# Last layer: two of eight channel blocks multiplied by the tokens' factors on POOL, six on VectorE

## The reference, cut to what matters

```python
def act_quant(x):
    scale = 127.0 / jnp.clip(jnp.max(jnp.abs(x), axis=-1, keepdims=True), 1e-05)
    return jnp.clip(jnp.round(x * scale), -128, 127) / scale
def bit_linear(x, w):
    ...
    return jnp.einsum('bsd,hd->bsh', xq, wq)
h = bit_linear(x, w1)
h = depthwise_conv1d(h.transpose(0, 2, 1), conv_w, conv_b)
h = h.transpose(0, 2, 1)
h = jax.nn.silu(h)
return bit_linear(h, w2)
```

## Time and profile before

| | us |
|---|---|
| median of 3 runs | 2888.92 |
| lowest, highest | 2888.0, 2890.59 |
| the profiled execution, device time | 2885.63 |
| its span in the trace | 2883.9 |
| DVE busy in the span | 1946.5 |
| PE busy | 2387.5 |
| POOL busy | 815.9 |

### The profile page before, as it was taken

The page is one execution under the profiler, slowest core; times in us unless marked ns, Lnnn a source line. Parts: engine busy times, 40 slices in busy tenths (PEclk is TensorE's granted clock), DMA queues, the critical chain, the costliest instruction groups (busy, mean ns, idle before and its releaser), DMA issues. The chain is left out here.

```text
span 2883.9 us, 43402 instructions
## 1 busy us (share of the span) xinstructions
PE 2387.5 (83%) x16438; PEld 1959.8 (68%) x16438; DVE 1946.5 (67%) x4381; ACT 1510.7 (52%) x2574; POOL 815.9 (28%) x712
## 2 busy tenths in 40 slices
PE   4778888876689999999868999999999367777665
PEld 2445555554477888888758999999999346464544
DVE  4688888875566656667545666666665358787867
ACT  3456777754445655656434554555544155455543
POOL 3233434432222434444440000000000563526030
PEclk9788988877799999999988999999999699989887
DMA  8400000000100111000014433443332421111000
GB/s 273 183 1 17 16 9 8 9 8 8 35 13 1 43 34 40 29 24 24 20 55 137 135 121 121 133 149 122 121 126 94 145 66 45 60 40 59 1 16 15
DMA packets 152518, 184.14 MB, mean 64 GB/s; under 512 B 21512, under 2 KB 118005, under 8 KB 152312
## 3 DMA queue, kind: packets, MB, share of 16 engines
q1 hardware_dynamic: 139304, 154.11, 16.3%
q0 software_dynamic: 12288, 27.15, 3.0%
q10 hardware_dynamic: 720, 0.12, 0.0%
HBM read 116.33 MB, written 71.43 MB: 65 GB/s over the span
## 5 line engine op out<-in xcount | busy, mean ns | idle before, releaser
L2409 POOL DMA_INDIRECT picked<-expert_out,so x128 | 126.4, 987 | 846.2 <-DMA so<-slots 743.3
L161 PE MATMUL SC<-Xhi,Whi 128*128 128x320 f32 x1024 | 320.4, 313 | 3.9 <-DVE Xlo L2204 2.5
L161 PE MATMUL SC<-Xlo,Whi 128*128 128x320 f32 x1024 | 317.5, 310 | 0.0
L161 PE MATMUL SC<-Xhi,Wlo 128*128 128x320 f32 x1024 | 317.5, 310 | 0.0
L641 POOL TENSOR_TENSOR PR<-PR,rs 128x616 f32<-128x616 f32 x128 | 162.8, 1272 | 388.8 <-DVE rs L1035 388.8
L1410 POOL TENSOR_TENSOR ff_Hlo<-ff_HF,ff_Hhi 128x512 fp32r<-128x512 f32 x108 | 142.8, 1322 | 389.0 <-ACT ff_Hhi L1543 388.9
L2185 ACT ACTIVATE SG<-SC 128x320 f32<-128x320 f32 x256 | 111.9, 437 | 239.6 <-PE SC L161 238.6
L161 PEld LDWEIGHTS SC<-Xhi,Whi 128*128 128x128 f32 x1024 | 193.3, 189 | 4.8 <-issue 2.8
L2218 DVE TENSOR_TENSOR Hlo<-HF,Hhi 128x320 fp32r<-128x320 f32 x256 | 125.5, 490 | 104.1 <-ACT Hhi L2173 104.1
L161 PEld LDWEIGHTS SC<-Xlo,Whi 128*128 128x128 f32 x1024 | 193.3, 189 | 0.0
L161 PEld LDWEIGHTS SC<-Xhi,Wlo 128*128 128x128 f32 x1024 | 192.9, 188 | 0.0
(11 more groups left out here) (495 smaller groups left out, 6958.7 us busy)
## 6 DMA issues: line engine op xcount, KB each, us to landing
expert_in<-zeros SPq DMA_DIRECT2D x4, 5120.0 KB, 32.3
rowsin<-expert_in SPq DMA_DIRECT2D x32, 640.0 KB, 5.9
expert_out<-rowsout SPq DMA_DIRECT2D x32, 640.0 KB, 4.0
first_expert<-L_wg SPq DMA_DIRECT2D x16, 512.0 KB, 6.8
first_expert<-L_wu SPq DMA_DIRECT2D x16, 512.0 KB, 7.0
first_expert<-L_wd SPq DMA_DIRECT2D x16, 512.0 KB, 7.8
Wraw<-L_wg SPq DMA_DIRECT2D x16, 512.0 KB, 7.0
Wraw<-L_wu SPq DMA_DIRECT2D x16, 512.0 KB, 7.2
```

Of the source, the lines that this page charges most:

```text
L161: last = nc.tensor.matmul(out, lhs[l], rhs[r], start=start and n == 0, stop=stop and n == 2)
L2409: nc.gpsimd.indirect_dma_start(picked[g][:, t, k, :], None, oute[:, :], bass.IndirectOffsetOnAxis(ap=so[g][:, t, k:k + 1], axis=0)).then_i ...
```

## The change

For each half, DVE multiplies blocks 0 to 3 as before and of the high blocks only 4 and 5 (1024 columns); POOL multiplies blocks 6 and 7 (LENT = 2, 1024 columns), in place in the same tile, as soon as the factors of the half are there. A new semaphore, scaled, makes DVE wait for POOL ahead of the rounding of the high blocks. The roundings and all other work stay as they were. POOL's two instructions stand at the end of its batch loop, behind the gathers.

```diff
+    LENT = 2
...
+                        for g in range(G):
+                            lent = SL[:, NHC - LENT:, g * TOK:(g + 1) * TOK]
+                            pool.wait_ge(sm["s2_ready"][g], b + 1)
+                            nc.gpsimd.tensor_tensor(lent, lent, bc_at(S2B[:, g * TOK:(g + 1) * TOK], 1, LENT), ALU.mult).then_inc(sm["scaled"][g], 1)
...
+                            mid = SL[:, HALF:NHC - LENT, tok]
                             dve.wait_ge(sm["s2_ready"][g], b + 1)
                             tt(low, low, by, ALU.mult)
-                            link(tt(high, high, by, ALU.mult))
+                            link(tt(mid, mid, bc_at(S2B[:, tok], 1, HALF - LENT), ALU.mult))
                             tsc(SQ[:, 0:HALF, tok], low, MAGIC, MAGIC, ALU.add, ALU.subtract)
+                            dve.wait_ge(sm["scaled"][g], b + 1)
                             tsc(SQ[:, HALF:, tok], high, MAGIC, MAGIC, ALU.add, ALU.subtract).then_inc(sm["q_ready"][g], 1)
```

More of the change, by code:

```diff
@@ L2325, in layer_3 @@
                 "y_psum", "y_taken", "xqt_psum", "sx_ready", "xr_ready", "xq_ready", "xq_high", "xq_low", "h_psum", "z0_ready", "z_ready", "s_ready",
-                "am_ready", "tile_psum", "tile_taken", "s2_psum", "s2_ready", "q_ready", "o_psum", "o_ready",
+                "am_ready", "scaled", "tile_psum", "tile_taken", "s2_psum", "s2_ready", "q_ready", "o_psum", "o_ready",
                 "diag_ready", "c_psum", "c_taken", "x_bias")}
```

## The result

The changed kernel takes 2893.11 us (median of 20 runs), the kernel before 2888.14 us in as many. The ratio is 1.0017, 95% interval 1.0011 to 1.0024: slower, by 5.0 us (3.2 to 6.9, which is 0.11% to 0.24%).

A forecast was written before the change was run, and what follows sets the result against it. VectorE (DVE) was taken to bound the four stretches. Per half, +2.16 us for POOL less 1.06 us removed gives +1.10; eight halves +8.8 us, waits and clock 0: 2888.92 + 8.8 = 2897.7 us, range 2892.5 to 2902.5 us.

The forecast's parts named there:

- The place and the path: Four stretches from first multiplication to last rounding, 13.69 us the first: DVE alone sets their length and the next batch's start.
- The removed part: DVE's second multiplication, halved to 1024 columns, falls from 2.286 to 1.23 us: 1.06 us less per half, eight times.
- The exclusion and its size: POOL's multiplication and DVE's work on SBUF run one after the other, adding 2.16 us per half (bounds 2.16 and 2.35).
- Who goes first, and the turns: At the stretch's start POOL goes a hair ahead, then engines alternate; half 0 gets both POOL turns, ending 3.3 us later.
- Added waits: POOL's wait for the factors and DVE's wait for POOL before the second rounding cost 0.
- side by side: Rival: POOL's multiplication runs beside DVE's at full speed in the stretches; -8.5 us, 2880.4 us; chance 7%.
- DVE keeps POOL out: Rival: POOL gets in only when DVE stops before the second rounding; +11.9 us, 2900.8 us; chance 13%.
- the clock rises: Rival: TensorE's clock rises enough at the boundaries, or delay is partly absorbed; 2889 to 2894.5 us; chance 22%.
- main case: In the stretches, POOL's turns add more than DVE's shorter multiplication saves; +6 to +11.5 us, 58%.
- the term for TensorE's clock: Clock change at the three batch boundaries, behind TensorE's idle 4.67 us: taken as 0, bounds -3 to +5 us.
- Hidden at the end?: TensorE's later second product of half 0 stays hidden before DVE's release, at the lower clock only by 2 us.
- Slower by over 0.2%: Whole kernel slower by more than 5.8 us, about what a measurement can tell from no change; 81%.

The follow-up runs named there:

- e3: Changed kernel without POOL's multiplication and DVE's wait for it (blocks 6 and 7 rounded without factors); 0.9975 of the kernel before.
- e5: Changed kernel with POOL's multiplication replaced by a fill of the same blocks that reads nothing from SBUF; 0.9974 of the kernel before.
- e6: Changed kernel with DVE reading factors from PSUM, POOL's half 1 after half 0's roundings, and scores and second product reordered; 0.9962 of the kernel before.
- e1: Kernel before plus unread TensorE products filling its idle time at the three batch boundaries and ahead of the last second product; 0.9985 of the kernel before.

## Why the prediction was right, and where it was off

- **The place and the path**: right. L243 follows the last rounding at once, before and after, and the +2.20 us arrive in the next batch.
- **The removed part**: 1.06 us per half expected, 1.07 measured (e3). Of the two rows for the short instruction, L1122's 1.23 us was the longest of eight (1.174 is usual); L1976's fits what came, 1.22.
- **The exclusion and its size**: right, 2.16 us per POOL turn expected, 2.17 measured; e5 and e6 show that it is the two engines' reading, since with either of them reading less both run at their own length. By the words that the prediction quotes from the Trainium skill (they stand in "SBUF — State Buffer", Summary: rules for kernel authors) it would have been 2.35 us; the traces bear out the early start instead. The net +1.10 us per half is what the stretches show, 15.81 - 13.61 = 2.20 for two.
- **Who goes first, and the turns**: right in each step: POOL ahead by 0.02 us, 4.48 us for the first multiplication (4.5 forecast), 3.36 for the short one (3.3), half 0 ready 3.3 us later.
- **Added waits**: 0, right (e5; in the profile after, the four instructions of each half also follow each other without idle time).
- **The rivals**: side by side and DVE keeps POOL out are both refuted, by 4.48 us and by the turns. The third one, the clock rises, is the one that came, together with the main mechanism: 2893.11 us lies in its 2889 to 2894.5 us, and +5.0 us below the main case's +6 to +11.5. It had been given 22%, the main case 58%.
- **The step that failed is the term for TensorE's clock.** "I take 0 for the clock, and -3 to +5 us" was -5.5 us at the three boundaries (3 x 2.20 = 6.6 us in the stretches, 1.1 arrived), outside its own bounds. Two things were wrong. The sign could be had: I had the idle 4.67 us and the scores at 1.2 GHz in hand, and had worked out that the second product would move closer to them (0.96 us of idle time are left), and I treated the outcome as open. And the size: I counted only the score steps, 1.0 us (1.08, 1.05 and 1.08 measured at the three boundaries, and the same in e1), but later work of TensorE meets the lower clock in other places, which gave another 0.9, 1.0 and 0.4 us. That the clock does this, e1 and the rows show; how much it gives in these later places I could not have worked out from the rows, and no run here shows a way to forecast it.
- **Hidden at the end?** "Still ends before" holds for the three boundaries. At the end of the kernel the slow first product is not hidden: the last part is 2.89 us longer instead of 2.2. The term is +0.7 us.
- In all: 8.8 - 5.5 + 0.7 = 4.0 us, as the traces say, 5.0 by the medians; the forecast was 8.8. Slower was right, and the time lies at the lower end of the range (2892.5 to 2902.5 us), in part by luck: with before at 2888.14 instead of 2888.92 us, +4.0 us would give 2892.1 us, just outside. The prediction's own sign of being wrong, "the stretch is 15.9 us and the time moves by less than 5 us, in which case it is the clock", is met by the trace (4.0 us) and stands on the edge by the medians (5.0 us). It is luck too that the profiled execution took 2894.70 us where 2894.4 was forecast: 5.06 us of that had gone by ahead of the change. "Slower by over 0.2%" had 81%; the measured 0.17% lies below that bound, its interval on both sides of it.

## What to carry to other kernels

Before work is moved from VectorE to GpSimd, ask what each instruction in the overlap reads. Two SBUF inputs on VectorE, or one at double pace, against a GpSimd instruction that reads SBUF run one after the other, and then GpSimd's slower pace (2.34 us for what VectorE does in 1.22) is a plain loss; an operand that can be had from PSUM makes the same division a gain. When a change moves the idle time of TensorE, price the clock with it: here it was worth 5.5 us, more than the net effect of the edit, and filling the idle time gave the kernel before a like sum without the edit. Only the part right behind the moved idle time (about 1.1 us per boundary) could be priced from rows of before.

## What the runs showed of the hardware that I had not expected

A delay on VectorE can speed up the part behind it. In the changed kernel TensorE's second product of half 0 is slower (6.32 instead of 3.67 us) and harms nothing at the three boundaries, and as it lies closer to the scores these run at 2.4 GHz: boundary 1 is 2.20 us longer in the stretch and ends 0.23 us later in all. The reverse is at boundary 1 of e3: 2.14 us less in the stretch, and the product on the chain takes 4.59 us instead of 3.67.

A GpSimd fill of 1024 columns (0.95 us) and a VectorE multiplication on two SBUF inputs overlap at no cost to either, while a GpSimd multiplication of the same blocks costs VectorE 2.17 us. The Trainium skill states both ("SBUF — State Buffer", Who interferes with whom): VectorE's second input comes through the read interface that GpSimd reads by, and an instruction that only writes does not contend. The traces agree, except that the held instruction begins about 0.13 us before the other one's recorded end, and that behind a finished instruction the one that waits comes next, even if the other engine's queue is ready.
